# Wide attention with 64-wide heads: values folded with the output weights, probabilities turned in chunks of 128 rows

## The reference, cut to what matters

```python
q = (x @ Wq).reshape(B, S, HEADS, 64).transpose(0, 2, 1, 3)
k = (context @ Wk).reshape(B, L, HEADS, 64).transpose(0, 2, 1, 3)
v = (context @ Wv).reshape(B, L, HEADS, 64).transpose(0, 2, 1, 3)
attn = softmax(jnp.einsum('bhsd,bhld->bhsl', q, k) * 64 ** -0.5)
out = jnp.einsum('bhsl,bhld->bhsd', attn, v)
out = out.transpose(0, 2, 1, 3).reshape(B, S, HEADS * 64)
return out @ Wo + bo
```

## Time and profile before

| | us |
|---|---|
| median of 3 runs | 2421.75 |
| the runs | 2421.75, 2418.1, 2432.82 |
| span of the profiled execution | 2408.2 |
| PE busy in the span | 1980.2 (82%) |
| DVE busy | 1543.5 (64%) |
| ACT busy | 1111.0 (46%) |
| POOL busy | 989.2 (41%) |

### The profile page before, as it was taken

The page is one execution under the profiler, slowest core; times in us unless marked ns, Lnnn a source line. Parts: engine busy times, 40 slices in busy tenths (PEclk is TensorE's granted clock), DMA queues, the critical chain, the costliest instruction groups (busy, mean ns, idle before and its releaser), DMA issues. The chain is left out here.

```text
span 2408.2 us, 39264 instructions
## 1 busy us (share of the span) xinstructions
PE 1980.2 (82%) x14419; PEld 1400.9 (58%) x14419; DVE 1543.5 (64%) x3706; ACT 1111.0 (46%) x2201; POOL 989.2 (41%) x886
## 2 busy tenths in 40 slices
PE   5887799799999976854593898799589888879998
PEld 3666599667777754431592555567367566654443
DVE  6996522368787755969314885511598699866775
ACT  4886444244444432225331665423244567644443
POOL 3554165344443214647566741271675200112332
PEclk9997799899999988975796999899699999999999
DMA  3000478321112125979891100342231100012221
GB/s 113 1 2 2 146 242 245 103 70 59 59 56 75 37 67 178 327 255 309 264 325 53 26 12 1 128 126 78 68 122 49 41 2 2 2 36 75 80 80 48
DMA packets 138277, 238.45 MB, mean 99 GB/s; under 512 B 20755, under 2 KB 66748, under 8 KB 133970
## 3 DMA queue, kind: packets, MB, share of 16 engines
q1 hardware_dynamic: 114216, 173.65, 21.7%
q0 software_dynamic: 23872, 62.29, 9.2%
HBM read 161.89 MB, written 73.99 MB: 98 GB/s over the span
## 5 line engine op out<-in xcount | busy, mean ns | idle before, releaser
L432 POOL TENSOR_TENSOR L1x_soft<-L1x_soft,L1x_rinv 128x616 f32<-128x616 f32 x64 | 77.6, 1214 | 190.8 <-DVE L1x_rinv L355 190.7
L2153 ACT ACTIVATE L3f_hT<-banks,L3f_b 128x512 f32<-128x512 f32 x128 | 87.9, 687 | 136.9 <-PE banks L2172 130.1
L2098 DVE TENSOR_TENSOR L3f_hT<-L3f_hT,L3f_spread 128x512 f32<-128x512 f32 x128 | 99.8, 802 | 35.1 <-ACT L3f_hT L2153 32.7
L2185 PE MATMUL banks<-L3f_hT,L3f_w 128*128 128x512 f32 x256 | 121.4, 598 | 0.0
L2172 PE MATMUL banks<-L3f_xT,L3f_w 128*128 128x512 f32 x256 | 120.1, 593 | 0.6 <-PEq L730 0.6
L2663 POOL DMA_INDIRECT L0e_rows<-xn_rows,L0f_token_of x78 | 77.9, 999 | 98.0 <-issue 61.7
L887 POOL TENSOR_TENSOR L0x_soft<-L0x_soft,L0x_rinv 128x1232 f32<-128x1232 f32 x32 | 71.9, 2247 | 99.7 <-DVE L0x_rinv L812 99.7
L2982 ACT ACTIVATE L0e_hT<-banks,L0e_w 128x256 f32<-128x256 f32 x156 | 69.1, 473 | 88.3 <-PE banks L3025 88.3
L404 ACT COPY L1x_attnT<-banks 128x512 f32<-128x512 f32 x64 | 37.5, 585 | 148.2 <-PE banks L513 148.2
L2663 POOL DMA_INDIRECT L1h_rows<-xn_rows,L1f_token_of x72 | 73.9, 1026 | 77.8 <-POOLq L2416 46.7
L266 DVE COPY L1x_keys<-banks 128x308 f32<-128x308 f32 x112 | 52.0, 464 | 69.0 <-PE banks L461 68.9
(11 more groups left out here) (600 smaller groups left out, 5850.9 us busy)
## 6 DMA issues: line engine op xcount, KB each, us to landing
hidden<-L1h_hid SPq DMA_DIRECT2D x24, 768.0 KB, 5.0
L0e_w<-in_L0f_w SPq DMA_DIRECT2D x39, 320.0 KB, 4.7
L0e_w<-in_L0f_w SPq DMA_DIRECT2D x39, 258.0 KB, 3.8
L1x_flat_values<-L1x_staged SPq DMA_DIRECT2D x34, 256.0 KB, 2.0
L1x_vals<-L1x_flat_values SPq DMA_DIRECT2D x14, 616.0 KB
mixed<-L1m_out SPq DMA_DIRECT2D x32, 256.0 KB, 4.0
L3f_spread<-L3f_gates SPq DMA_DIRECT2D x8, 1024.0 KB, 7.4
L3x_keys<-L_keys SPq DMA_DIRECT2D x5, 1232.0 KB
```

Of the source, the lines that this page charges most:

```text
L432: pool.tensor_tensor(tile, tile, rinv[n % 2][:, :].unsqueeze(2).to_broadcast([P, U, NK]), ALU.mult).then_inc(probs_ready, 1)
L2098: dve.tensor_tensor(tile, tile, spread[t % 2][:, e, :], ALU.mult).then_inc(weighed, 1)
L2153: act.activation(hT[m % 3][:, c, :], hid_bank[(FC * m + c) % 4][:, :], ACT.Relu, bias=b1[:, FC * e + c:FC * e + c + 1]).then_inc(hid_out, 1)
L2185: last = pe.matmul(bank[:, :], w2[:, e, c, :], hT[m % 3][:, c, :], start=False, stop=(e == E - 1 and c == FC - 1))
```

## The change: what it does

For each head the value weights (96x64) and the output weights (64x128) are multiplied once, ahead, into `vo` (96x128). Values of a head are then 128 wide and already in the output's space, so `wo`, `attnT` and `proj_bank` go: the value matmuls add up in `out_bank[:, 0:128]` over heads, and DVE adds that to `x`. The probabilities of a unit (8 heads x 77 = 616 columns) are turned as one flat row: four chunks of 128 (one copy on ACT) and a rest of 104, which is a job `r` through the preparation banks; five matmuls of 128x128 replace the eight of 77x64. The keys of a head are copied by ACT. A `v` job still makes 512 columns, which are now four heads instead of eight, so there are twice as many (L1x 72 for 36; L3x 12 flat jobs for 8 by batch).

The values go to HBM in a layout by batch, unit and flat row (head, key), so that they come back in chunks of 128 rows: five loads a unit. A flat `v` tile of 128 context rows is cut where a batch begins, and each piece is a store of its own, in runs of 128 floats (512 B). Both L1x and L3x use this way now. `KeysAhead` makes six `v` jobs a piece for four, and stores a piece by seven transfers for two; the products, `a` and `vo`, are made in L0f and L1f alone and kept. `Early` issues three loads a piece for two. The numbers given to the routes change: L0f from (1 piece, 3) to (12 jobs, 7), L1f (1, 12) to (18, 0), L2f (1, 3) to (14, 3). In the mix ACT does two jobs in every step from 1 on.

The core of the diff:

```diff
+def flat_segments(lo, hi):
+    found = []
+    for batch in range(lo // NKEY, -(-hi // NKEY)):
+        a, b = max(lo, batch * NKEY), min(hi, (batch + 1) * NKEY)
+        found.append((a - lo, b - lo, batch, a - batch * NKEY, b - batch * NKEY))
+    return found
+
+def load_values(sp, kept, out, t, u, sem):
+    for b in range(4):
+        sp.dma_start(out[:, u, b, 0:CHUNKS - 1, :],
+                     kept["vals"][4 * t + b, u, 0:P * (CHUNKS - 1), :].rearrange("(c p) d -> p c d", p=P)).then_inc(sem, 16)
+    sp.dma_start(out[0:REST, u, :, CHUNKS - 1, :],
+                 kept["vals"][4 * t:4 * t + 4, u, P * (CHUNKS - 1):U_KEYS, :].rearrange("b p d -> p b d")).then_inc(sem, 16)
...
-        values_of = [[("v", (f, c)) for f in flat_tiles[t] for c in range(HU)] for t in range(NTURN)]
+        values_of = [[("v", (f, c)) for f in flat_tiles[t] for c in range(2 * HU)] for t in range(NTURN)]
...
+            if place == 1 and 0 <= n - 2 < NU:
+                found.insert(0, ("r", n - 2))
...
+            if what == "r":
+                act.copy(probsT[j % 2][0:REST, CHUNKS - 1, :], bank[0:REST, 0:P]).then_inc(act_out, 1)
+                return
+            if what == "k":
+                act.copy(keys[t % 2][:, jobs_of[t][j][1], :, :],
+                         bank[:, 0:4 * NK].rearrange("p (b k) -> p b k", b=4)).then_inc(act_out, 1)
+                return
...
             if i >= S:
-                act.wait_ge(v_stored[i % S], 16 * (i // S))
+                act.wait_ge(v_stored[i % S], 16 * sum(len(places[k]) for k in range(i % S, i, S)))
             act.copy(staged[i % S][0:m, :], bank[0:m, :]).then_inc(act_out, 1)
...
-                last = pe.matmul(bank[0:m, :], flat_context[:, P * f:P * f + m], wv[:, 512 * c:512 * c + 512],
+                last = pe.matmul(bank[0:m, :], flat_context[:, P * f:P * f + m], vo[:, 4 * c:4 * c + 4, :],
...
-                    sp.dma_start(flat_values[c, P * f:P * f + rows_of(f), :], staged[k % S][0:rows_of(f), :]).then_inc(v_stored[k % S], 16)
+                    for p0, p1, batch, k0, k1 in places[k]:
+                        sp.dma_start(kept["vals"][batch, c // 2, :, :].rearrange("(h k) d -> k h d", k=NK)[k0:k1, c % 2 * 4:c % 2 * 4 + 4, :],
+                                     staged[k % S][p0:p1, :].rearrange("p (h d) -> p h d", h=4)).then_inc(v_stored[k % S], 16)
...
-        sp.dma_start(self.kept["vals"][t, u, :, :, :], self.vals[k % self.sets][:, :, :]).then_inc(self.stored[k % self.sets], 16)
+        for f in range(3):
+            lo, m = self.rows(t, f)
+            for p0, p1, batch, k0, k1 in flat_segments(lo, lo + m):
+                sp.dma_start(self.kept["vals"][batch, u, :, :].rearrange("(h k) d -> k h d", k=NKEY)[k0:k1, :, :],
+                             self.vals[k % self.sets][p0:p1, f, :].rearrange("p (h d) -> p h d", h=8)
+                             ).then_inc(self.stored[k % self.sets], 16)
...
-                for k, begin in ((0, 1), (1, 9)):
-                    if begin <= p < begin + 6:
-                        ahead.act_piece(act, k, range(2 * (p - begin), 2 * (p - begin) + 2))
+                if p >= 1:
+                    ahead.act(act, 2 * (p - 1), 2 * p)
```

More of the change, by code:

```diff
@@ L2361, in act_products @@
-    def act_products(self, act):
-        for i in range(self.rounds):
-            act.wait_ge(self.products_ps, i + 1)
-            for odd in range(2):
-                act.copy(self.a[:, 8 * i + odd:8 * i + 8:2, :],
-                         self.banks[odd][0:CTX, :].rearrange("p (h d) -> p h d", h=4)).then_inc(self.a_out, 1)
-    def pe_piece(self, pe, k):
-        t, u = self.pieces[k]
-        if k == 0:
-            pe.wait_ge(self.a_out, 2 * self.rounds)
-        for j in range(12):
-            n = 12 * k + j
-            bank = self.banks[n % 2]
+        products = [(i, odd) for i in range(heads // 8 if raw else 0) for odd in range(2)]
@@ new lines, in pe, with rows, pe_product @@
+                lo_row, m = self.rows(t, f)
+                flat = self.net.context[:, :, :].rearrange("p b k -> p (b k)")
+                last = pe.matmul(bank[0:m, :], flat[:, lo_row:lo_row + m], self.w["vo"][:, 8 * u + 4 * c:8 * u + 4 * c + 4, :],
+                                 start=True, stop=True)
+            last.then_inc(self.made, 1)
+    def rows(self, t, f):
+        lo, hi = 4 * NKEY * t + P * f, min(4 * NKEY * t + P * (f + 1), 4 * NKEY * (t + 1))
+        return lo, hi - lo
+    def pe_product(self, pe, n, what, i):
+        left, right = (self.raw["wkT"], self.raw["wqT"]) if what == "a" else (self.raw["wvT"], self.raw["wo"])
+        if n:
+            pe.wait_ge(self.out, n)
+        for c in range(4):
+            for odd in range(2):
+                rows = slice(64 * odd, 64 * odd + 64)
+                last = pe.matmul(self.banks[(n + odd) % 2][0:CTX, c * P:(c + 1) * P], left[rows, 4 * i + c, :],
+                                 right[rows, 4 * i + c, :], start=True, stop=True)
+                if c == 3:
+                    last.then_inc(self.made, 1)
@@ L2632, in _ @@
         def _(pe):
-            if ahead:
-                ahead.pe_products(pe)
-            for k in range(first):
-                ahead.pe_piece(pe, k)
+            ahead.pe(pe, 0, first)
             pe.wait_ge(made, 1)
@@ L2646, in _ @@
             last.then_inc(ranks_ps, 1)
-            for k in range(first, pieces):
-                ahead.pe_piece(pe, k)
+            ahead.pe(pe, first, len(ahead.jobs))
             for b in range(B):
@@ L3184, in _ @@
         def _(pe):
-            ahead.pe_products(pe)
-            for k in range(2):
-                ahead.pe_piece(pe, k)
+            ahead.pe(pe, 0, len(ahead.jobs))
         @block.sync
@@ L3497, in build @@
                                          kept=kept1, ready=READY_1, early=early)
+                folded("L3x", 4, w3, ahead, "right")
                 route(nc, net, "L1f", 24, 86, routed, logits,
-                      dict(w=w3, heads=8, kept=kept3, pieces=[(t, 0) for t in range(2)]), 1, 12, chosen)
+                      dict(w=w3, raw=raw3, heads=8, kept=kept3, pieces=[(t, 0) for t in range(2)]), 18, 0, chosen)
             passing.close()
```

324 lines of the change are left out of this document (151 added, 173 removed).

## The result

The changed kernel takes 2521.74 us (median of 4 runs, 2518.1 to 2525.38) where the kernel before takes 2423.84 (median of 4, 2418.1 to 2432.82). The comparison of the single runs gives 1.0414 times the time, 95% interval [1.0382, 1.0446]; the quotient of the two medians is 1.0404. The forecast was 2530, slower. The profiled execution took 2525.38 us with a span of 2523.6, so the span leaves out 1.8 us. If that holds for before too, its profiled execution, with a span of 2408.2, was some 14 us quicker than its median, and quicker than each of its four runs; the spans differ by 115.4 us, the medians by 97.9.

What follows compares the result with a forecast made beforehand. PE was taken to bound L1x, DVE then PE L3x, DVE and DMA together the mix. Terms -37+100+21+7+5+0+13+2 = +111 us, added to the median 2421.75, gave 2530 us, range 2400 to 2600.

Steps and rivals of the forecast that it cites:

- What bounds L1x: L1x: PE, busy 47.93 of 50 us, counts nearly in full at 6.2 us a unit; other engines don't take over.
- Part 1: L1x: PE saves 80 us on units and gains 39 of `v` jobs; -37 us net, 5.6 us a unit.
- Part 2: L1x: stores of 53, 71 or 73 rows use one DMA engine, 29 ns a run; ACT waits, +100 us.
- The loads' share: L1x: the next turn's first stores queue behind ten loads; a quarter of 7·9.3 us counted, 17 us.
- the signs: L1x profile: long ACT waits in turns 2, 4, 7; PE well under 47 of 50; DMA share near 0.2.
- Part 3: L3x: PE's work -5, fetches of values +4, stores of turns 6 and 7 +22; +21 us together.
- Part 4: Routes: changed copies and products on ACT and PE give L0f +7, L1f +5, L2f 0 us.
- Part 5: Mix: stores of values load one DMA engine and ACT waits for piece 0's, +13 us; Early's loads +2.
- Stores through all engines: Whole kernel: stores use all engines or land before ACT is back; -12 us, 2410, chance 0.18.
- PE's gain alone: Whole kernel: stores quick, and the routes' and mix's additions hide behind DVE; 2384 us, chance 0.09.
- One engine at 20 ns: Stores: one engine alone is quicker, or few-engine stores fall on different engines; +34 us, 2456, chance 0.15.
- The clock: L1x, turns 2, 4, 7: TensorE's clock falls in stalls, up to 45 us more; 2600 and over, chance 0.08.

Runs made afterwards that it cites:

- run 7: The changed kernel with stores cut at a multiple of 16 rows, four staged tiles, and keys copied by DVE instead of ACT: 2459.45 us, 1.0154.
- run 9: The kernel before with the keys of a head copied by ACT instead of DVE, nothing else: 2402.34 us, 0.9916.
- run 10: The changed kernel with values ordered by key, then head (whole stores), the order made by POOL, two staged tiles: 2396.93 us, 0.991.
- run 5: The changed kernel with values ordered by key, then head, the order made by POOL, three staged tiles instead of two: 2387.69 us, 0.9866.
- run 8: The kernel before with its L1x stores of values cut where a batch begins, still in runs of 2048 B: 2418.15 us, 0.9986.
- run 2: The changed kernel with the flat row ordered by key, then head, DVE writing and summing with a stride: 2444.95 us, 1.0078.
- run 6: The changed kernel with stores cut at a multiple of 16 rows and four staged tiles instead of two: 2420.08 us, 0.9985.

## Why the prediction was right, point by point

**What bounds L1x: right, but for one thing.** PE's work counts nearly in full, but the prediction gave the key copies nothing, because DVE had about 5 of 6.2 us. Runs 7 and 9 show them worth 39 and 18 us: what counted was where they stand in DVE's list, as DVE was under 80% busy.

**Part 1, PE -37: PE's work right, and the time right only because the copies moved.** With whole stores and two tiles (run 10) PE is busy 326.1 us from the first exponent to the last, where before has 363.6, -37.5, and L1x takes 349.2 us, 35.2 less. But that gain needs the key copies on ACT. With them on DVE and the stores cut and quick (run 7) PE's work falls too, and L1x is no shorter than before:

```profile
468.90:853.30 384.40, 363.60 (x2628) 273.71 (x2630) 289.66 (x743) 170.88 (x307) 155.87 (x141) 0.98 0.18 57
```

```profile
484.60:874.30 389.70, 342.18 (x1660) 233.75 (x1660) 291.66 (x742) 137.27 (x282) 155.50 (x140) 0.96 0.42 101
```

(the first is the kernel before, the second run 7: PE idles 47.5 us for 20.8.) The copies alone give 19.9 in the kernel before (run 9), so the two parts don't simply add. In the changed kernel the gain shows nowhere, since its best turn is 48.2 us, not the 45 that was said to show in turns 1 and 5. That step is wrong as put: in turn 5 ACT waits 8.8 us for the first store, which SP issues at 738.2, behind turn 4's last stores and ten loads, and turn 1 takes 49.9 us even in run 5.

**Part 2, stores +100 in L1x: the mechanism right, the price too high, two terms missing.** Between run 10 and the changed kernel, which differ in the shape of the stores and in POOL's order, L1x differs by 91.5 us. The number of engines carries it: cutting at 16 rows took 55 us from L1x with the same bytes and runs. Where a store of 71 rows runs alone, the rate is that of one engine, 0.07 at 22 GB/s, and in run 8 two of them under way at once ran one after the other. The run costs 23 ns, not 29. Between the prediction's own bounds (40 us at 20 ns, 100 at 29) that makes some 60, an estimate by a straight line. The loads' share in it, a quarter of 9.3 us a turn and 17 in all, was low: in turns 3, 5 and 6 alone the first stores behind the loads held ACT for 22 us.

On PE the 91.5 us split into 57.9 more idle and 33.6 more busy with the same 1655 records. The 33.6 is PE at a clock of 0.87 for 0.99, and the most that the clock can have cost. It was a rival's mechanism, there on top of the forecast; it worked inside the forecast's stalls, and the sum had no term for it. The other thing that the sum did not have is SP's hold: that SP issues a store in 0.32 us "and is not the limit" was wrong, with a median issue of 1.68 us in the longest stall. The hold is part of the idle time; how much of it the hold adds to the engine's own time no run tells. That the +100 came near 91.5 is thus in part luck. Of the signs, the long waits came in the turns named, and PE fell well under 47 of 50 (53.29 of 74.40 us in the turn of tile 17); the DMA share did not stay near 0.2, it is 0.28 to 0.42 in the later turns shown. When a single store lands the trace does not say; 284 runs at 23 ns are 6.5 us, an estimate inside the 6 to 10 named.

The rule of the Trainium skill (page "DMA: Bandwidth & Descriptors", section "Why a DMA increments its semaphore by 16 and not by 1") that SP's transfers take the lowest-numbered engines puts all one-engine stores on one engine. No row of before could show that; run 8's two stores, one after the other at 28 and 26 GB/s, agree, though the trace does not name the engine.

**Part 3, L3x +21: measured +12.9.** Run 10 has 162.3 us there, so the stores and what hangs on them cost 17.0 of the forecast 22 + 4, and the rest of the change gave 4.1 of the forecast 5. The turn with tile 17 (34.9 us for 23.9) has 11 of it.

**Part 4, routes +12: about right in sum.** L0f and what lies ahead of it +9.5 (forecast +7), L1f +2.8 (+5), where the ranks came 5.1 us later, as forecast, and half was given back behind them. L2x and L2f, forecast 0, took 12.0 more. Of these L2f, from the first instruction of its `high` tile, has only 1.8 (46.0 us for 44.2); the other 10.2 lie in L2x. In L2x, which the change does not touch, PE is busy 177.70 us for 172.10 with the same thousand matmul records, at clock 0.84 for 0.86:

```profile
1278.00:1508.00 230.00, 172.10 (x1008) 111.42 (x1008) 157.07 (x610) 120.48 (x356) 120.65 (x101) 0.86 0.08 19
```

```profile
1369.00:1605.00 236.00, 177.70 (x1007) 114.46 (x1007) 156.79 (x610) 120.68 (x356) 120.67 (x101) 0.84 0.08 19
```

(the first is the kernel before, the second the changed one). L2x takes 251.7 us before, 256.9 in run 8 and 258.8 in run 9, whose L2x and L2f are the code of before; the runs with the change have 255.1 to 263.1 (261.9 in the changed kernel). So a good part of the 10.2 is the profiled execution of before, the quickest of all, and not the change; whether the change adds to the rest stays open.

**Part 5, the mix +13: measured +17.5,** by the mechanism named: with quick stores and the new order (run 2) it is gone. In run 6, whose pieces are stored as in the change, it stays (120.2). What counted was ACT's wait of 21.2 us in the step right behind piece 0; in the forecast it stood beside the time on a DMA engine without a price of its own.

**The rivals.** Stores through all engines: run 10, with two tiles and whole stores, is nearest to what that rival describes: 2397 and not 2410, with L1x, L3x and the mix each some 5 or 6 us better than its sum. PE's gain alone, 2384: the routes' additions did not hide. One engine at 20 ns, 2456: nearer to the true price (23) than the forecast, and off because the price was not the only cost. The clock: true as a mechanism, at most 33.6 of the 45 that it allowed for in L1x, and contained in the result.

So the forecast of +111 against +97.9 measured (+115.4 between the profiled executions) was right for its main reason, the divisors of the row counts; that the size came so near was partly luck, a price too high standing in for a fallen clock and a held SP.

## What to carry to other kernels

Count the rows of every transfer before its bytes: a cut at a natural border (77 keys) that leaves 53 or 71 rows turns a transfer of sixteen engines into one of a single engine, and a layout whose tiles are whole blocks (here by key, then head) costs nothing where the engine that reorders has room. Ask for an eviction not only how busy its engine is but what stands behind it in that engine's list; 39 us lay in moving copies between two engines that were both under 80% busy. When a change mixes a gain and a loss, undo the loss alone before judging the idea: the same change with whole stores, the order made by POOL and a third tile is 1.3% faster than the kernel before.

## What the runs showed of the hardware that was not expected

- An issue on SP, 0.32 us before, lasted up to 7.36 us when one-engine stores of 284 runs queued, and small stores behind it could not start; with stores of 71 runs (run 8, tile 17) it stayed at 0.34 and less.
- Two one-engine stores under way at once moved at the rate of one engine, 28 and 26 GB/s in runs of 2048 B, one after the other (run 8).
- DVE wrote 616 floats a row with a stride of 8 elements in 1.28 us and summed over that stride in 1.25, against 0.80 and 0.78 dense; POOL's product written with the same stride took 1.32 against 1.21. The Trainium skill, page "SBUF — State Buffer", section "Door 1: The DMA port swizzle (why `[64,N]` ≈ `[32,N]`)", says that each access to a new 16-byte line pays; DVE's rows agree, and POOL's show how little of it is seen there.
- The granted clock fell to 0.50 within L1x itself, in the stalls of 17 us and less. Over the stage it was 0.87 where run 10 has 0.99, and the same 1655 matmul records took PE 33.6 us longer.
